# Squares of fields in rows of two instead of four in a factorisation-machine tower (CIN) on one core

## The reference, cut to what matters

```
Wr  = W.reshape(O, Hj, 32)
nxt = einsum('bjk,bzk,ojz->bok', h, e, Wr) + b     # h = e in the first layer
h, o = nxt[:, :64], nxt[:, 64:]                    # layers 0 and 1; layer 2: o = nxt
z   = concatenate of the o, summed over k          # then relu(z' @ W_top1), relu(@ W_top2), @ W_top3
```

## Time and profile before

| what | us |
|---|---|
| three timed runs | 664.99, 665.00, 667.02; median 665.0 |
| the profiled execution's own time | 666.33 |
| its span (first to last instruction) | 664.6 |
| PE busy | 627.3 (94%) |
| DVE busy | 484.8 (73%) |
| ACT busy | 213.1 (32%) |

### The profile page before, as it was taken

The page is one execution under the profiler, slowest core; times in us unless marked ns, Lnnn a source line. Parts: engine busy times, 40 slices in busy tenths (PEclk is TensorE's granted clock), DMA queues, the critical chain, the costliest instruction groups (busy, mean ns, idle before and its releaser), DMA issues.

```text
span 664.6 us, 32262 instructions
## 1 busy us (share of the span) xinstructions
PE 627.3 (94%) x14488; PEld 520.8 (78%) x14488; DVE 484.8 (73%) x491; ACT 213.1 (32%) x351; POOL 128.9 (19%) x137
## 2 busy tenths in 40 slices
PE   5844899999999999999999999999999999999998
PEld 5833588888888888888888888888888888888773
DVE  4237788888888888888888888888888888851000
ACT  2330333444433333333333333333333333332012
POOL 7755044445443544100000000000000000000000
PEclk9686899999999999999999999999999999999999
DMA  5110011111111111100000000000000000002000
GB/s 180 30 28 17 14 24 28 28 25 32 26 25 24 29 26 27 20 15 13 12 12 12 12 12 12 12 12 12 12 12 12 12 12 12 12 18 65 11 1 0
DMA packets 31658, 14.87 MB, mean 22 GB/s; under 512 B 24177, under 2 KB 28897, under 8 KB 31378
## 3 DMA queue, kind: packets, MB, share of 16 engines
q1 hardware_dynamic: 27442, 10.26, 7.2%
q0 software_dynamic: 4192, 4.25, 2.9%
HBM read 8.03 MB, written 0.00 MB: 12 GB/s over the span
## 4 chain that ended last, share of the span: by engine, by line
PE 89%; POOL 5%; issue 3%; DVE 2%; DMA 1%; ACT 0%; DVEq 0%; POOLq 0%
PE psX L335 20%; PE psT L392 20%; PE psT L416 8%; PE psT L402 7%; PE psT L376 7%; PE psT L379 6%; POOL G_sb L239 5%; PE psX L379 4%; PE psX L376 4%; PE psX L346 3%; PE psX L466 2%; PE psX L355 1%; PE psX L273 1%; PE psT L480 1%; PE psX L496 1%
## 5 line engine op out<-in xcount | busy, mean ns | idle before, releaser
L392 PE MATMUL psT<-T_sb,W1d 64*64 64x256 f32 x1024 | 234.3, 379 | 0.0
L396 PE MATMUL psT<-T_sb,W1d 64*64 64x256 f32 x1024 | 234.3, 379 | 0.0
L402 PE MATMUL psT<-T_sb,W1d 64*64 64x256 f32 (+3 forms) x2048 | 205.3, 300 | 0.0
L684 DVE TENSOR_TENSOR prod<-X 128x1024 f32 (+4 forms) x202 | 170.7, 914 | 15.5 <-PE psT L379 15.3
L721 DVE STREAM_TRANSPOSE PT<-prod 128x4608 f32<-128x4608 f32 x32 | 159.0, 4969 | 0.0
L392 PEld LDWEIGHTS psT<-T_sb,W1d 64*64 64x64 f32 x1024 | 131.3, 133 | 27.8 <-issue 14.4
L335 PE MATMUL psX<-PT,W0T 32*64 32x256 f32 x4608 | 136.0, 382 | 12.5 <-DVE PT L721 9.1
L335 PEld LDWEIGHTS psX<-PT,W0T 32*64 32x64 f32 x4608 | 118.8, 134 | 32.9 <-issue 29.9
L416 PE MATMUL psT<-T_sb,W1d 64*64 64x64 f32 (+2 forms) x1536 | 141.7, 270 | 0.0
L396 PEld LDWEIGHTS psT<-T_sb,W1d 64*64 64x64 f32 x1024 | 131.3, 133 | 0.0
L402 PEld LDWEIGHTS psT<-T_sb,W1d 64*64 64x64 f32 x2048 | 123.6, 133 | 0.8
(11 more groups left out here) (78 smaller groups left out, 557.1 us busy)
## 6 DMA issues: line engine op xcount, KB each, us to landing
X<-T_sb SPq DMA_DIRECT2D x64, 64.0 KB, 2.0
kept<-grams SPq DMA_DIRECT2D x128, 16.5 KB
G_sb<-in_L_rec_W SPq DMA_DIRECT2D x2, 1024.0 KB, 4.8
E_q<-in_tbl,ids_g POOLq DMA_INDIRECT x96
prod<-in_W_top SPq DMA_DIRECT2D x2, 512.0 KB, 3.5
G_sb<-in_L_rec_W SPq DMA_DIRECT2D x1, 512.0 KB, 5.7
G_sb<-in_tbl,ids POOLq DMA_INDIRECT x32, 2.4
dT<-dT SPq DMA_DIRECT2D x3, 32.0 KB, 2.0
```

Of the source, the lines that this page charges most:

```text
L392: mm(psT[low, 0, 0:HF * SMP], W1d[low, HF + k, :], cross.rearrange("p v (z y) s -> p v z y s", y=HF)[:, :, :, k, :], start=start, stop=sto ...
L396: mm(psT[high, 0, 0:HF * SMP], W1d[low, k, :], T_flat[low, SMP * row:SMP * (row + HF)], start=start, stop=stop, tile_position=(0, C))
L402: last = mm(out[:, SMP * 4 * a:], W1d[high, HF * v + k, :], T_flat[high, SMP * (row + 4 * a):SMP * (row + HF)], start=start, stop=stop and ...
L684: return tt(out, x[:, :, z0:z0 + nz].unsqueeze(3).broadcast_to(shape), x[:, :, y0:y0 + ny].unsqueeze(2).broadcast_to(shape), ALU.mult)
```

## The change

The stored part of the squares is cut finer: eight blocks of two fields instead of four of four. Of row z only columns y from 2a on are kept (a = z // 2), 16+14+...+2 for the eight blocks, times two rows: 144 columns (D_COLS) instead of 160. ROW and SHIFT change with it; the first five blocks lie at a regular distance of 14 columns (REGULAR), the last three do not. With the 16 columns of the fields the row is now exactly 288 = 9 x 32 columns, so the blocks that are transposed are the whole row; the field columns get weights of zero in W0_sym, and h keeps its 9 blocks.

```diff
-D_COLS, L_COLS = 160, 128
+D_COLS, L_COLS = 144, 128
-PROD = X_AT
-BLOCKS = PROD // Q
-ROW = 40
-SHIFT = (0, 12, 24, 16)
+BLOCKS = HALF // Q
+ROW = 72
+SHIFT = (0, 14, 28, 42, 56, 48, 32, 16)
+REGULAR = 5
@@ g2_matmuls
-                    a, i = k // 4, k % 4
+                    a, i = k // 2, k % 2
                     for v in range(2):
-                        last = mm(out[:, SMP * 4 * a:], W1d[high, HF * v + k, :],
-                                  T_flat[high, SMP * (row + 4 * a):SMP * (row + HF)],
+                        last = mm(psT[C * v:C * v + C, 1, SMP * 2 * a:SMP * HF], W1d[high, HF * v + k, :],
+                                  T_flat[high, SMP * (row + 2 * a):SMP * (row + HF)],
-                    if a:
+                    regular = min(a, REGULAR)
+                    for b, n in [(0, regular)] * (a > 0) + [(b, 1) for b in range(REGULAR, a)]:
                         for v in range(2):
+                            first = SHIFT[b] + k
+                            if n == 1:
+                                moving = rows[:, :, first, :]
+                            else:
+                                moving = rows[:, :, first:first + SHIFT[1] * (n - 1) + 1:SHIFT[1], :]...
-                            last = mm(out[:, 0:SMP * 4 * a], W1d[high, HF * v + k, :], moving,
+                            last = mm(psT[..., 1, SMP * 2 * b:SMP * 2 * (b + n)], W1d[high, HF * v + k, :], moving,
@@ W0_sym
+                nc.vector.memset(half[:, X_AT:HALF], 0.0)
-                for a in range(4):
+                for a in range(HF // 2):
@@ products
-                for a in range(4):
-                    square(e, a, x, by_half[e][:, :, 0:D_COLS], 4 * a, HF - 4 * a)
+                for a in range(HF // 2):
+                    square(e, a, x, by_half[e][:, :, 0:D_COLS], 2 * a, HF - 2 * a)
@@ transposes
-                return nc.vector.transpose(PT[:, :].rearrange("p (u c) -> p u c", c=PROD),
-                                           by_half[e][:, :, 0:PROD])
+                return nc.vector.transpose(PT[:, :], prod[:, SMP * HALF * e:SMP * HALF * (e + 1)])
```

More of the change, by code:

```diff
@@ L78, in dlrm_tower @@
         grams = sb("grams", [P, 4, GRAM])
-        PT = sb("PT", [P, SMP * PROD])
+        PT = sb("PT", [P, SMP * HALF])
         PT_blocks = PT[:, :].rearrange("p (t b r) -> p t b r", t=TILES, r=Q)
@@ L113, in dlrm_tower @@
         W2_b1 = T_flat[:, 0:2048].rearrange("p (i z) -> p i z", z=NF)
-        W0_sym = T_flat[0:C, 2048:2048 + 2 * PROD]
+        W0_sym = T_flat[0:C, 2048:2048 + 2 * HALF]
         d_raw = T_flat[:, 2624:2624 + GROUPS * DENSE].rearrange("p (g d) -> p g d", g=GROUPS)
@@ L126, in dlrm_tower @@
         y_sb = T_flat[0:1, 4096:4608]
-        z0_high = T_flat[0:C, 4608:5120]
+        z0_high = prod[0:C, 2176:2688]
         psT = ps("psT", [P, 4, BANK])
@@ L397, in g2_matmuls @@
                        start=start, stop=stop, tile_position=(0, C))
-                    a, i = k // 4, k % 4
+                    a, i = k // 2, k % 2
                     for v in range(2):
-                        out = psT[C * v:C * v + C, 1, 0:HF * SMP]
                         row = D_COLS * v + ROW * i + SHIFT[a]
-                        last = mm(out[:, SMP * 4 * a:], W1d[high, HF * v + k, :],
-                                  T_flat[high, SMP * (row + 4 * a):SMP * (row + HF)],
+                        last = mm(psT[C * v:C * v + C, 1, SMP * 2 * a:SMP * HF], W1d[high, HF * v + k, :],
+                                  T_flat[high, SMP * (row + 2 * a):SMP * (row + HF)],
@@ L404, in g2_matmuls @@
                                   start=start, stop=stop and not a, tile_position=(C, C * v), skip_group_check=True)
-                    if a:
+                    regular = min(a, REGULAR)
+                    for b, n in [(0, regular)] * (a > 0) + [(b, 1) for b in range(REGULAR, a)]:
                         for v in range(2):
-                            out = psT[C * v:C * v + C, 1, 0:HF * SMP]
-                            at = D_COLS * v + k
                             rows = T_flat[high, SMP * D_COLS * v:SMP * D_COLS * (v + 1)]\
-                                .rearrange("p (i w s) -> p i w s", i=4, s=SMP)
-                            if a == 1:
-                                moving = rows[:, :, k, :]
+                                .rearrange("p (i w s) -> p i w s", i=2, s=SMP)
+                            first = SHIFT[b] + k
+                            if n == 1:
+                                moving = rows[:, :, first, :]
@@ L413, in g2_matmuls @@
                             else:
-                                moving = rows[:, :, k:k + SHIFT[1] * (a - 1) + 1:SHIFT[1], :]\
+                                moving = rows[:, :, first:first + SHIFT[1] * (n - 1) + 1:SHIFT[1], :]\
                                     .rearrange("p i b s -> p b i s")
-                            last = mm(out[:, 0:SMP * 4 * a], W1d[high, HF * v + k, :], moving,
-                                      start=False, stop=stop, tile_position=(C, C * v), skip_group_check=True)
+                            last = mm(psT[C * v:C * v + C, 1, SMP * 2 * b:SMP * 2 * (b + n)], W1d[high, HF * v + k, :],
+                                      moving, start=False, stop=stop, tile_position=(C, C * v), skip_group_check=True)
@@ L661, in _ @@
             for v in range(2):
-                squares = W0_sym[:, PROD * v:PROD * v + D_COLS].rearrange("p (i w) -> p i w", w=ROW)
-                for a in range(4):
[L664 to L669, removed]
+                half = W0_sym[:, HALF * v:HALF * (v + 1)]
+                nc.vector.memset(half[:, X_AT:HALF], 0.0)
+                squares = half[:, 0:D_COLS].rearrange("p (i w) -> p i w", w=ROW)
+                for a in range(HF // 2):
+                    z0 = HF * v + 2 * a
+                    at = SHIFT[a] + 2 * a
+                    cp(squares[:, :, at:at + 2], w0[:, z0:z0 + 2, z0:z0 + 2])
+                    if a < HF // 2 - 1:
+                        sym(squares[:, :, at + 2:SHIFT[a] + HF], z0, 2, z0 + 2, HF - 2 * a - 2)
+                last = sym(half[:, D_COLS:X_AT].rearrange("p (z y) -> p z y", y=HF),
                            8 * v, 8, HF, HF)
@@ L693, in square @@
                 rows = out.rearrange("p u (i w) -> p u i w", w=ROW)
-                return times(rows[:, :, :, SHIFT[a] + y0:SHIFT[a] + y0 + ny], x, 4 * a, 4, y0, ny)
+                return times(rows[:, :, :, SHIFT[a] + y0:SHIFT[a] + y0 + ny], x, 2 * a, 2, y0, ny)
             def x_of(e, first_tile):
@@ L731, in _ @@
                 out = by_tile[0][:, :, v, 0:D_COLS]
-                for a in range(4):
-                    y0, y1 = max(4 * a, 8 * (q % 2)), 8 * (q % 2) + 8
+                for a in range(HF // 2):
+                    y0, y1 = max(2 * a, 8 * (q % 2)), 8 * (q % 2) + 8
                     if y0 < y1:
```

## The result

The changed kernel takes 673.69 us (median of 4; 671.34 to 675.07) against 665.0: ratio 1.0132, 95% interval 1.0098 to 1.0167. The forecast was 671.7, and slower. Its profiled execution took 674.17 (span 672.5), 7.84 more than the one before; the forecast was +6.7.

A forecast was written before the change was run, and what follows sets the result against it. The prediction took PE's own time per step, by pass distances in the fullest quarter, as the bound. t -12.2, g2 +18.7 and first products +0.25 made +6.7 us: 671.7 from 665.0, range 666 to 680.

The forecast's parts named there:

- g2's +0.584 us a step: In g2's high quarters, new 32-column passes at 57.5 ns each lengthen the stage: +18.7 us over 32 steps.
- The first part: g2 for k 0 to 3, before the h transposes: forecast to grow by 0.123 us a step.
- t's -0.381: In t, 288 instead of 320 columns and shorter copies save 0.381 us a step: -12.2 us over 32 steps.
- tile 7's own 53: In t, the last tile's two shorter passes were to give 53 ns a step, part of the 381 ns.
- The floor itself, 57.5 ns: In g2, the weight load sets the distance behind a 32-column pass: 57.5 ns instead of 29 by columns.
- Rows 9: Profile rows of g2's high quarters: 128-column passes 109 ns apart, 64-column passes 57.5, read as already touching the floor.
- Rows 11: Profile rows at the kernel's end: 64-column passes with 128 columns of weights stand 121 ns apart, read as a floor.
- Rival A: In g2, the load doesn't bind and a 32-column pass costs its columns, 29 ns: 653.6 us, faster; chance 0.13.
- L: Theory that the weight load sets a floor of some 58 ns behind a pass in g2's high quarters.
- B: In g2, the load costs more than at 64 columns: 67 ns a pass, 677.8 us; chance 0.09.
- D: In g2, part of the load is hidden: a pass near 47 ns, break-even at 665 us; chance 0.06.
- C: In t, ACT's and DVE's copies set the pace and the change gives nothing: +18.9, 683.9 us; chance 0.03.

The follow-up runs named there:

- the cuts at 64, 32 and 16 columns: Kernel before, own-row multiplication of fields k = 1 to 10 in g2 cut in two, last 64, 32 or 16 columns apart: 670.65, 685.66, 693.67 us.
- the lower multiplications taken out: Changed kernel with one lower multiplication per field also for a = 6 and 7 (reads wrong columns): 660.14 us against 665.48 for the kernel before.
- t's multiplications alone: Kernel before with 288 instead of 320 moving columns for the squares in t, copies still 128x640: 656.12 us against 666.13.

## Why the prediction was right

- PE's distances in the fullest quarter as the measure: right. The loss in PE's passes against the gain in PE's passes gives the result; ACT and DVE count only with the two small terms that the sum gave them, the shorter copies (0.07 us a step, forecast 0.061) and the first products (+0.21 us, forecast 0.25).
- g2's +0.584 us a step: measured +0.545. Shown by the cuts at 64, 32 and 16 columns (g2 +0.11, +0.61, +0.86 us a step) and by the lower multiplications taken out. The first part was 0.025 too dear: the last two passes before the h transposes are the pair of which only 28 ns show, and nothing behind them in g2 pays it back.
- t's -0.381: measured -0.35 alone and -0.32 in the changed kernel, where tile 7 starts 0.315 us earlier instead of 0.328. Half of tile 7's own 53 ns does not come out, as in the run with t's multiplications alone, and the next h starts 0.022 us later behind t's last pass. What sets that start was not found.
- The floor itself, 57.5 ns: right (58), by one sound row and one misread. Rows 9 carried it. Rows 11 were read as a load of 121 ns with 128 columns of weights; the load is 112 and hidden under the slow reading of scattered numbers. That half of 121 is near 58 was luck. The rule of the Trainium skill ("TensorE: Matmul & The Clock Gate", section "LDWEIGHTS (loading the stationary operand)", P / 1.2 ns) gives 107 and 53; the runs have 112 and 58, 5 more each, so the 121 that the prediction set beside the 107 was not the load.
- The prediction also let a load start only when the pass before has started, for every pass. Behind a long pass one load is ready earlier (28 ns); this moves passes inside a k and hardly its sum.
- Rival A, passes at their columns, fell with the cuts at 32 and 16; at 64 it is too near L to tell. The Trainium skill's rule that the prediction quoted with it ("TensorE: Matmul & The Clock Gate", section "Back-to-back issue gap"), an issue floor of some 25 ns for up to 64 columns, does not hold here where each pass has a load of its own: 58 ns at 16, 32 and 64 columns. Rivals B (67 ns), D (47 ns) and C (t gives nothing) fell too.
- Not in the prediction: h's late loads through the place of the second loop's code, +0.087 us in a late step and 2.6 us in all, and 0.4 us before the first h. In the profiled pair the misses add up to what was measured: 6.7, h +2.6, t +1.9, g2 -1.25, the start +0.35 and the clock's two steps -2.4 make 7.9, against 7.84. That the total came so near is in part luck, since these terms have both signs; the medians lie 8.7 apart, 2 us more than forecast, and which of the terms these 2 us are they can't tell.

## What to carry to other kernels

Before cutting a multiplication, compare its columns with its weights' columns. Here a pass of f32 with fewer moving columns than its weights have costs its weight load, 58 ns with 64 columns of weights and 112 with 128, and a finer cut saves nothing there (transposes apart). A saving in one stage that forces short passes in another can be had in full if the pieces are chosen anew, here by symmetry and a negative step. And a row that seems to show a cost must differ from its neighbour in that one thing only: rows 11 differed in the weights and in how far apart the numbers lay.

## What the runs showed of the hardware that was not expected

- A pass on f32 numbers 136 bytes apart takes 1.9 ns a column instead of 0.83, and that hides the weight load (123 ns where the load is 112).
- The first short pass behind a long one is followed after 28 to 29 ns, and a later pass comes as much later: one weight load seems to be had ahead.
- The quarters keep no common order: passes of the low quarters for one k start before the last ones of the high quarters for the k before (437.20 and 437.29), and they stand up to 0.40 us apart when the high quarters fall behind.
- The same loop body takes 17.03, 17.12 or 17.17 us with 48, 0 or 16 more instructions ahead of the loop (one execution each), by weight loads that come 0.17 to 0.18 us late behind its jump.
